# A new order for the last attention slot and the first two expert steps of a fused network on one Trainium2 core, with step 0's masked pairs rounded by ScalarE

## The reference, cut to what matters

```python
x = x + L0_xattn(layernorm(x), ctx, ctx)
x = x + gelu(layernorm(x) @ W1) @ W2            # W1, W2 composed from low-rank primitives
x = x + L1_xattn(layernorm(x), ctx, ctx)        # softmax(Q K^T / sqrt(D)) V Wo
x = x + L1_ffn(layernorm(x))

def L1_ffn(x):
    logits = gelu(x @ w_r1 + b_r1) @ w_r2 + b_r2
    top_p, top_i = top_k(softmax(logits), 2)            # 2 of 8 experts per token
    integrated, v = x, 0
    for _ in range(2):
        ctx = concat([integrated, v])
        shared = inl(gelu(ctx @ w_s1 + b_s1) @ w_s2 + b_s2, integrated, v)
        expert = inl(gelu(ctx @ w1[top_i] + b1) @ w2[top_i] + b2, integrated, v)
        x_next, v = mix(shared, weighted sum of expert over the 2)
        halt = sigmoid(gelu(x_next @ w_h1 + b_h1) @ w_h2 + b_h2)
        refined = gelu(x_next @ w_f1 + b_f1) @ w_f2 + b_f2
        integrated = integrated + halt * refined * integration_weight
    return integrated
```

## Time and profile before

| | |
|---|---|
| median of 3 runs | 349.97 us (349.29 to 350.16) |
| the profiled execution | 348.92 us |
| its span, first to last instruction | 347.1 us |
| PE busy (matmuls) | 317.9 us, 92% |
| DVE busy | 263.5 us, 76% |
| ACT busy | 192.9 us, 56% |
| POOL busy | 36.5 us, 11% |
| mean granted TensorE clock | 0.985 |

### The profile page before, as it was taken

The page is one execution under the profiler, slowest core; times in us unless marked ns, Lnnn a source line. Parts: engine busy times, 40 slices in busy tenths (PEclk is TensorE's granted clock), DMA queues, the critical chain, the costliest instruction groups (busy, mean ns, idle before and its releaser), DMA issues.

```text
span 347.1 us, 4339 instructions
## 1 busy us (share of the span) xinstructions
PE 317.9 (92%) x1482; PEld 224.9 (65%) x1490; DVE 263.5 (76%) x529; ACT 192.9 (56%) x303; POOL 36.5 (11%) x47
## 2 busy tenths in 40 slices
PE   4989999899899458899899999999999999999995
PEld 4764697555465336567576777767777777776763
DVE  1474844558656776798969988999996996999693
ACT  3410024366936643497877966777556746545743
POOL 0030012122020203103710020000000000000000
PEclk9989999999989899999999999999999999999999
DMA  7999940000000000015263154001001000000001
GB/s 265 428 423 293 313 190 0 0 3 1 0 2 0 0 1 2 0 60 136 48 181 60 62 144 85 16 0 32 0 0 28 5 0 1 32 0 20 12 0 60
DMA packets 13172, 25.20 MB, mean 73 GB/s; under 512 B 608, under 2 KB 9056, under 8 KB 11872
## 3 DMA queue, kind: packets, MB, share of 16 engines
q1 hardware_dynamic: 11712, 20.75, 16.7%
q0 software_dynamic: 1440, 4.19, 6.5%
HBM read 16.55 MB, written 1.05 MB: 51 GB/s over the span
## 4 chain that ended last, share of the span: by engine, by line
PE 74%; DVE 14%; ACT 6%; issue 4%; DMA 1%; DVEq 0%; ACTq 0%
PE ps L1346 70%; DVE ring L1014 1%; PE ps L1444 1%; ACT ring L533 1%; ACT L533 1%; DMA pA<-in_packA 1%; DVE st L801 1%; PE ps L1560 1%; PE ps L1463 1%; DVE wz L1014 1%; DVE a L817 1%; PE ps L1433 1%; DVE ring L948 1%; DVE xtok L1001 1%; DVE ring L956 1%
## 5 line engine op out<-in xcount | busy, mean ns | idle before, releaser
L1346 PE MATMUL ps<-hm_even,ew_hi 128*128 128x512 f32 (+1 forms) x152 | 48.6, 418 | 1.4 <-issue 1.4
L1346 PE MATMUL ps<-hm_odd,ew_hi 128*128 128x512 f32 (+1 forms) x148 | 47.1, 421 | 0.0
L1346 PEld LDWEIGHTS ps<-hm_even,ew_hi 128*128 128x128 f32 (+1 forms) x152 | 26.4, 188 | 6.4 <-issue 1.5
L585 ACT ACTIVATE hid<-ps,pB 128x512 f32<-128x512 f32 x32 | 21.7, 688 | 14.4 <-PE ps L1346 13.8
L1346 PEld LDWEIGHTS ps<-hm_odd,ew_hi 128*128 128x128 f32 (+1 forms) x148 | 25.6, 189 | 5.5 <-issue 0.5
L1346 PE MATMUL ps<-hm_even,ew_lo 128*128 128x512 f32 (+1 forms) x72 | 25.3, 392 | 0.0
L431 POOL TENSOR_TENSOR zz<-zz,mhalf 128x4 f32<-128x4 f32 x12 | 12.4, 1034 | 100.3 <-DVE zz L906 100.3
L1346 PE MATMUL ps<-x_hi,w1x_hi 128*128 128x512 f32 x40 | 18.8, 470 | 4.2 <-DVE xtok L1001 3.6
L1346 PE MATMUL ps<-hm_odd,ew_lo 128*128 128x512 f32 (+1 forms) x64 | 22.3, 394 | 0.0
L1014 DVE SCALAR_TENSOR_TENSOR ring<-ring,pB,hid 128x1024 f32<-128x1024 bf16 x16 | 20.5, 1282 | 0.8
L525 ACT ACTIVATE hB<-ps 128x512 f32<-128x512 f32 x16 | 9.6, 597 | 19.8 <-PE ps L1346 19.8
(11 more groups left out here) (324 smaller groups left out, 757.3 us busy)
## 6 DMA issues: line engine op xcount, KB each, us to landing
ring<-in_fc1b SPq DMA_DIRECT2D x4, 1024.0 KB, 17.2
ring<-in_fc2a SPq DMA_DIRECT2D x4, 1024.0 KB, 7.4
hm_odd<-hm_odd SPq DMA_DIRECT2D x4, 512.0 KB, 3.5
packC<-in_packC SPq DMA_DIRECT2D x1, 1152.0 KB, 9.1
pB<-in_packB SPq DMA_DIRECT2D x1, 1077.0 KB, 8.7
ctxT<-in_ctxT SPq DMA_DIRECT2D x2, 512.0 KB, 6.3
xtok<-in_xtok SPq DMA_DIRECT2D x1, 1024.0 KB, 8.7
xT<-in_xT SPq DMA_DIRECT2D x1, 1024.0 KB, 10.7
```

The source lines that it names most:

```text
L585: act.activation(hid[:, j, :], hid_bank(s, j), ACT.Gelu, bias=W("eb1", j, j + 1)).then_inc(sem("hid"), 1)
L1346: return pe.matmul(out, lhsT, rhs, start=start, stop=stop)
```

## The change

The slots keep their work, but slots 2 and 3, step 0 and step 1 are reordered on all four engines:

- **Step 0 moves into slot 3.** `expand(0)` and the hidden tiles j = 1, 3 and 0 now stand between slot 3's own products; the rest of attention chunk 3 (`probs_t(3)`, `att_v(3)`, `router1(2)`, `router2(2)`) moves into `controls(0, BETA)`, and all of `expand(1)`, `ln_tok("rt", 3)`, `center(3)` and step 1's hidden tiles move into `controls(0, GATE)`. `expand_weights(0)` and `expand(2)` come after it. In step 1 `hidden(2, (0, 1))` and `expand_weights(1)` move too.
- For that, routing goes by chunks (0), (1, 2), (3) instead of (0, 1), (2, 3). There are three calls of `route`, `second_exp` and `weigh`, the last `second_exp` in step 1 after beta.
- **Rounding.** Step 0's three masked pairs are rounded by ScalarE (`mask_high`, Copy 128x1024), and `x_hi` of steps 0 and 1 too (`state_high`). VectorE keeps the subtraction.
- Banks: the router uses banks 4, 4, 0, 6, and the scores no longer wait for the logits; `ffn_down(3)` does.
- The roundings of w1x, wf1, wh1 and wh2 move from slot 1 to slot 0 on ScalarE, and their low parts from slot 2 to slot 0 on VectorE.

No arithmetic is added to or taken from any engine's products. The core of the diff:

```diff
-            return {0: (1, 2, 0, 3, HT), 1: (1, 0, 2, 3, HT)}.get(s, tuple(range(HT + 1)))
+            return {0: (1, 3, 0, 2, HT), 1: (1, 0, 2, 3, HT)}.get(s, tuple(range(HT + 1)))
@@ banks @@
-            return (bank[7], bank[7], bank[4], bank[1])[c]
+            return (bank[4], bank[4], bank[0], bank[6])[c]
+        def att_bank(c):
+            return bank[7] if c == NCH - 1 else bank[5]
+        def tok_bank(n):
+            return bank[6] if n == 3 * NCH - 1 else bank[n % 2]
+        def routed(c):
+            return (1, 2, 2, 3)[c]
@@ gpsimd @@
-            weigh(0)
...
-                    weigh(2)
...
+                if n == LN["att", 3]:
+                    weigh(0, 1)
...
+                if s == 1:
+                    weigh(1, 2)
+                if s == 2:
+                    weigh(3, 1)
@@ scalar @@
             for t in range(NCH):
...
+                if t:
+                    gelus(t, range(FT))
+                if a:
+                    exps(t - 1)
...
+                if t == 3:
+                    second_exp(0, 1)
+                if q:
+                    center_evac(t - 2)
+                if t == 2:
+                    r1_gelu(0)
...
+                    state_high(0)
+            def mask_high(j):
+                act.wait_ge(sem("hm"), hm_at(0, j))
+                act.activation(high_of(0, j), hm[j % 2], ACT.Copy).then_inc(sem("hhi"), 1)
+            expand_evac(0, 2, 3)
+            hidden_gelus(0, (1, 3))
+            r1_gelu(1)
+            hidden_gelus(0, (0,))
+            mask_high(1)
+            exps(3)
+            center_evac(2)
+            hidden_gelus(0, (2, HT))
+            mask_high(3)
+            state_high(1)
+            mask_high(2)
+            r1_gelu(2)
+            squashed(0, BETA)
+            expand_evac(1, 7, 6)
+            hidden_gelus(1, (1,))
+            center_evac(3)
+            hidden_gelus(1, (0, 2))
+            r1_gelu(3)
+            hidden_gelus(1, (3, HT))
+            weights_evac(0, 7, 6)
+            expand_evac(2, 7, 6)
+            state_high(2)
+            squashed(0, GATE)
+            second_exp(1, 2)
...
                 squashed(s, BETA)
+                if s == 1:
+                    second_exp(3, 1)
                 refine1(s - 1)
@@ vector @@
             def lower(s, j):
                 if j:
-                    high(s, j)
+                    if s:
+                        high(s, j)
...
                 if s == 1:
                     kept(s, 2)
                     high(s, 2)
+                    ln_scale("rt", 3)
                     lower(s, 1)
                     kept(s, 3)
                     high(s, 3)
+                    logits(3)
                     lower(s, 0)
                     state_split(s + 1)
                     slot_masks(s + 1)
                     shared_halves(s)
+                    route(3, 1)
...
+            kept(0, 1)
             att_scores(3)
             att_max(3)
+            att_add(2)
+            logits(1)
+            lower(0, 1)
             ln_stats("rt", 2)
+            kept(0, 3)
+            att_norm(3)
+            lower(0, 3)
+            att_pt(3)
             ln_scale("rt", 2)
             kept(0, 2)
             lower(0, 2)
+            lower(0, 0)
+            shared_halves(0)
             att_add(3)
             logits(2)
+            route(1, 2)
+            state_split(1)
             ln_stats("rt", 3)
             slot_masks(1)
             kept(1, 1)
@@ tensor @@
-                ffn_down(t, (2, 3))
+                ffn_down(t, (2,))
+                if t == 3:
+                    pe.wait_ge(sem("fh"), FT * NCH)
+                    expand(0, 2, 3)
+                ffn_down(t, (3,))
...
+                if t == 3:
+                    hidden(0, (1,))
+                if a:
+                    probs_t(t - 1)
+                ln_tok("att", t, "x2")
+                scores(t)
+                if t == 3:
+                    hidden(0, (3,))
                 if q:
                     router1(t - 2)
                 if a:
-                    probs_t(t - 1)
+                    att_v(t - 1)
+                if t == 3:
+                    hidden(0, (0,))
                 if q:
                     router2(t - 2)
-                ln_tok("att", t, "x2")
-                scores(t)
-                if a:
-                    att_v(t - 1)
             ln_tok("rt", 2, "x3")
             center(2)
+            hidden(0, (2, HT))
             ln_spread("rt", 2)
...
+                    controls(0, BETA, between={5: attended, 3: valued})
+                    controls(0, GATE, between={2: expand_1, 3: hidden_1, 4: hidden_0, 5: hidden_2, 6: hidden_3})
+                    router2(3)
+                    hidden(1, (HT,))
+                    expand_weights(0, 7, 6)
+                    expand(2, 7, 6)
...
-                controls(s, BETA, between={1: {5: hidden_rest, 6: expand_3, 13: weights_1},
+                controls(s, BETA, between={1: {3: hidden_first, 5: hidden_rest, 13: expand_3},
                                            2: {3: hidden_rest, 5: weights_2, 6: weights_3}}.get(s, {}))
+                if s == 1:
+                    weights_1()
```

More of the change, by code:

```diff
@@ L418, in _, with link, weigh @@
             pool.tensor_tensor(rstd[:, :], veps[:, :], mhalf[:, :], ALU.pow).then_inc(sem("rstd"), 1)
+            pooled = [0]
+            def link(ins):
+                pooled[0] += 1
+                ins.then_inc(sem("pool_chain"), 1)
+                pool.wait_ge(sem("pool_chain"), pooled[0])
+            def weigh(c, n):
+                t = slice(c * BPC, (c + n) * BPC)
+                pq, sq = pq_2[:, :, 0:n * BPC], sq_2[:, :, 0:n * BPC]
+                pool.wait_ge(sem("de"), routed(c))
+                pool.wait_ge(sem("first"), routed(c))
+                link(pool.tensor_scalar(pq[:, 1, :], rt[:, 6, t], 1.0, None, ALU.add))
+                link(pool.tensor_tensor(pq[:, 0, :], pq[:, 1, :], minus_1[:, 0:n * BPC], ALU.pow))
+                link(pool.tensor_tensor(pq[:, 1, :], rt[:, 6, t], pq[:, 0, :], ALU.mult))
+                link(pool.tensor_scalar(pq, pq, swc[:, 4:5], None, ALU.mult))
+                link(pool.tensor_tensor(sq, pq, rt[:, 5, t].unsqueeze(1).to_broadcast([128, 2, n * BPC]), ALU.mult))
+                link(pool.tensor_tensor(pq, pq, sq, ALU.subtract))
+                for k in range(2):
+                    pool.tensor_tensor(cf2[:, k, t], sq[:, k, :], pq[:, 1 - k, :], ALU.add)\
+                        .then_inc(sem("cf2"), 1)
+                pool.wait_ge(sem("cf2"), 2 * routed(c))
             pool.wait_ge(sem("rstd"), 1)
@@ L727, in last_halt @@
                     .then_inc(sem("lth"), 1)
[L729 to L738 removed]
+            for s in range(1, STEPS):
                 if s + 1 < STEPS:
@@ L1636, in _ @@
                     ffn_up(t, (3,))
+                if q:
+                    center(t - 2)
                 ffn_down(t, (0, 1))
@@ L1648, in _ @@
                 if a:
-                    probs_t(t - 1)
+                    att_v(t - 1)
+                if t == 3:
+                    hidden(0, (0,))
                 if q:
                     router2(t - 2)
-                ln_tok("att", t, "x2")
-                scores(t)
-                if a:
-                    att_v(t - 1)
             ln_tok("rt", 2, "x3")
             center(2)
-            pe.wait_ge(sem("fh"), FT * NCH)
-            expand(0, 2, 3)
-            hidden(0, (1, 2))
+            hidden(0, (2, HT))
             ln_spread("rt", 2)
-            hidden(0, (0, 3))
-            probs_t(3)
-            router1(2)
-            att_v(3)
-            hidden(0, (HT,))
-            router2(2)
-            ln_tok("rt", 3, "x3")
-            center(3)
-            pe.wait_ge(sem("hid"), HT)
-            expand(1, 3, 5)
             pe.wait_ge(sem("bp"), 1)
@@ L1746, in controls @@
                 late = s == 1 and rows_last
-                for i in (1, 3, 5, 2, 4, 6) if n == LAST else range(1, NT):
+                for i in (1, 3, 5, 2, 4, 6) if n == LAST else (1, 2, 5, 6, 3, 4) if n == 0 else range(1, NT):
                     if i in between:
@@ L1853, in hidden_rest, with hidden_first @@
                         refine_b(s - 2)
-                if s <= 2:
-                    hidden(s + 1, (0, 1))
-                elif s + 1 < STEPS:
+                def hidden_first():
+                    hidden(2, (0, 1))
+                if s == 2:
+                    hidden(3, (0, 1))
+                elif 3 <= s < STEPS - 1:
                     hidden(s + 1)
```

300 lines of the change are left out of this document (130 added, 170 removed).

## The result

| | before | after |
|---|---|---|
| median of the runs | 349.96 us (349.29 to 350.16) | 354.16 us (352.27 to 354.24) |
| ratio, 95% interval | | 1.0102 (1.0069 to 1.0135) |
| the profiled execution | 348.92 us | 354.24 us |
| its span | 347.1 us | 352.4 us |
| mean granted TensorE clock | 0.985 | 0.971 |

The change makes the kernel slower, by 1.0%. That is the side that the prediction took, but the time, 354.16, lies above its 351.3 and above the upper end of its range, 353.4.

A forecast was written before the change was run, and what follows sets the result against it. TensorE was taken as full from 180 us; its waits and slow clock between 82 and 180 us, some 19 us, were winnable. Walk -0.4 plus clock +1.7 gave +1.3: 349.97 + 1.3 = 351.3 us, range 348.2 to 353.4.

The forecast's parts named there:

- The walk at full clock: Slot 2 to halt_a of step 1, instruction by instruction with TensorE at full clock: 177.0 against 177.37, -0.4 us.
- The lead of 14 us: expand(0) starts at 104.5 instead of 118.79; waits for ScalarE and VectorE then eat this lead.
- the two long waits: TensorE waits 2.9 us at router1(3) for ln_scale, and 3.2 us at halt_a for the refinement's GELU.
- the charge for the clock: Half clock behind the waits at router1(3) and halt_a, up to 1.7 us each; one charged, +1.7 us.
- some 7 us in pieces: TensorE's waits in step 0 during ScalarE's chain up to 127.5; no clock loss charged for them.
- The rival that charges both long waits: Waits at router1(3) and halt_a both lose the clock: +3.0, 353.0 us; chance 0.11.
- The rounding: Step 0's masked pairs on ScalarE: 128x1024 rounding taken as 0.93 us to the next start, bounds 0.61 and 1.25.
- the rival of 0.61: ScalarE's step 0 chain 1.0 us shorter if a rounding costs 0.61: -1.4 with the clock up, 348.6 us; chance 0.24.
- Theory A: Experiments' theory: time went to half-clock stretches behind TensorE's waits, three on the path, some 4.5 us; the prediction charged 1.7.
- The table load: The new second_exp(3, 1) adds a load and an exponential to ScalarE's chain from weights_1 in step 1: +1.41 us.
- The rival with another 1.4 us behind each load: Each ScalarE table load costs more than its row: +2.7 on the forecast, 352.7 us; chance 0.05.
- POOL's `weigh(1, 2)`: Step 1, from the exponential at 158.1 to weights_1 at 167.7: 9.6 us for seven small operations, costed at nothing.

The follow-up runs named there:

- The changed kernel with its waits filled: Changed kernel plus products that nobody reads in four TensorE waits (step 0, router2(2), router1(3), halt_a): 349.35 us, ratio 0.9991 to before.
- the two filled kernels: Changed kernel with unread products in all four waits, 349.35 us, and only in the two ahead of router1(3) and halt_a, 351.15 us.
- the three moves: Changed kernel with second_exp(3, 1) ahead of weights_1's evacuation, chunk 3's scaling first on VectorE in step 1, logits(3) ahead of hidden tile 3's mask: 346.32 us, ratio 0.9915.

## Why the prediction was right, and where it was wrong

**The walk at full clock held.** It gave -0.4 us for the new order at full clock against the kernel before as it is. The changed kernel with its waits filled is at ratio 0.9991, -0.3 us. The lead of 14 us that waits eat up again, and the place and size of the two long waits came out: 2.9 and 3.2 us forecast, 2.78 and 3.15 measured. The kernel with its waits filled, which has no fall on the path, follows the walk mark by mark: forecast against measured there, slot 3 95.9 / 95.63, `router2(2)` 127.5 / 126.94, `expand(1)` 133.75 / 133.17, `router1(3)` 145.7 / 145.19, `expand(2)` 153.25 / 152.90, `weights_1` 167.7 / 167.76, `halt_a` 177.0 / 177.16.

```profile
133.17 0.62 PE L1385 MATMUL ps<-ident_h,tif 128*128 128x128 bf16 x8
...
177.16 0.50 PE L1385 MATMUL ps<-xn_hi,wh_hi 128*128 128x512 f32 x1 [0.42 <-ACT zz L715]
```

The sum alone, -0.4, is no change. That the kernel would be slower was forecast through the charge for the clock only, so the side was right for the right reason and the size of that charge was not.

**Its marks in the changed kernel.** Predicted against measured: slot 3 starts 95.9 / 96.70; `router2(2)` 127.5 / 128.13; `expand(1)` 133.75 / 135.93; `router1(3)` 145.7 / 147.93; `expand(2)` 153.25 / 157.10; first GELU of step 2 159.5 / 163.46; `weights_1` 167.7 / 171.97; `halt_a` 177.0 / 181.36. The lag grows in two steps, 1.6 us between `router2(2)` and `expand(1)` and 1.6 between `router1(3)` and `expand(2)`. Both lie on a fall of the clock, 126 to 138 and 144 to 160 us. Between the steps it hardly moves. Of the 0.8 at slot 3, some 0.45 is older than the change: the last products of the weights' composition, the same in both kernels, start at 40.50 us before and at 40.95 after, since the clock at 20 to 28 us was lower in this execution. `halt_a` is 3.99 us later than in the earlier trace rows, and the span 5.3 longer: the 1.3 between them are the fall behind `halt_a`, the third. Together 1.6 + 1.6 + 1.3 = 4.5 us, and 354.16 is 4.6 above the 349.6 of the walk without a fall.

**The step that failed is the charge for the clock.** It said that each of the two waits of about 3 us would cost up to 1.7 us and charged one. The size of one fall was right, 1.7 us. Their number on the path was three, and one of them came in step 0 behind waits of 1.0 to 2.1 us, for which the prediction had put nothing, since in the kernel before "the other waits had no such loss". It had even written "some 7 us in pieces" for these waits. They are 1.03, 2.12 and 0.97 us, 4.1 in all, and the fall behind them costs 1.5 us by the two filled kernels. The rival that charges both long waits gave 353.0 and came nearer, two falls for three. The earlier trace rows had the warning: one of the two falls before stood by a wait of 1.57 us. Short waits aren't always followed by one: those of 1.4, 0.7 and 1.6 us at the entrance of step 1 had full clock behind them in the changed kernel. The Trainium skill ("TensorE: Matmul & The Clock Gate", Part 1) has half rate as the default state, which activity releases; that alone does not say which waits are charged, as the prediction read it. The four falls behind waits agree with the page, and which waits draw one stays open here.

**The rounding was priced right and judged too little.** 0.93 us to the next start was forecast, 0.94 to 1.07 measured, so it was in the sum, and the rival of 0.61 fell. But the prediction never asked what the same order would do with VectorE rounding. By the traces it is 0.45 to 0.7 us shorter in step 0. The times are 0.6 us lower by the ratios with the waits filled, within the noise, and 1.9 with the three moves, most of that with the clock. Theory A, by which the engine of the rounding is a wash in the new order, missed its range for the time three times, once by 0.2 us. In the old order it is a wash.

**The table load** cost its row: 1.28, 0.20 and the next load at once (177.81 to 179.33), +1.5 against the 1.41 of the prediction. The rival with another 1.4 us behind each load fell. The Trainium skill ("ScalarE: Activation LUTs", What ACT_TABLE_LOAD costs) has that drain; the trace shows none. Put into an idle time of 2.19 us, the load and its exponential took nothing from the chain: `halt_a` came 1.6 us earlier.

**POOL's `weigh(1, 2)`**, costed at nothing, held with 1.2 us to spare. It ran from 162.25 to 170.74, and `weights_1` started at 171.97 without waiting for it.

**The account of the 1.0%.** By ratios to before: the new order takes 4.1 us for the clock where the old one takes 2.0, which makes 2.1, and at full clock it is 1.7 behind, of which the rounding on ScalarE is some 0.5 by the traces. What the rest is was not taken apart. The three moves show that two misplaced instructions on VectorE and one on ScalarE hid a gain: with them the new order is 0.9% faster than before, and with them and the old rounding 1.4%.

## What to carry to other kernels

When a reordering replaces one long wait of TensorE by several short ones, count half-clock stretches as a cost of each group of waits, not only of the long ones, and charge each that lies where TensorE is next on the path. Fill the waits with products that nobody reads, once for each order that is compared: the pair of times separates what the order does from what the clock does, if the traces show that the falls on the path are gone. Before giving up on a new order, look at every wait that it creates for an instruction that its engine could have done in an idle time just ahead; here three such moves turned +1.0% into -0.9%.
